# A batch's layer norm moved into the end of the scan stage, 64-row matmuls issued as halves, and one load delayed in the DMA queue

## The chip, the cores and the metric

One core of a Trainium2 chip runs the whole program. The metric is device time in microseconds (us), from start to end of one execution.

## What is computed

x has 4 batches of 64 channels and 32 x 32 positions (1024 tokens). Three parts follow one another, all in float32:

```python
# 1. two selective scans (forward, reversed), 128 inner channels, 16 states, for each of 4 batches
h = dA * h + (dt_t * x_t)[:, :, None] * B_t[:, None, :]   # over 1024 positions
y = jnp.einsum('bds,bs->bd', h, C_t)
y = _groupnorm_silu(y_f + y_b, gn_gamma, gn_beta) + x
# 2. causal attention over 1024 tokens, one head of 64
t = t + softmax(mask(q k^T / 8)) v,   q, k, v from layernorm(t)
# 3. spectral filter layer with hard expert choice (the first chosen expert adds up)
t = t + sum_k conv(layernorm(t), phi_k) (M_phi_plus_k, M_phi_minus_k) + 3 taps
```

## The kernel before, in words

The program has three blocks with a barrier between them; the order of work on each engine is written out by hand and tied by semaphores.

**Scan stage** (`mamba_stage`). A unit is one batch in one direction, so there are 8 units of 16 states. For a state the DMA queue (SP, `spread_b`, `spread_c`, line 388) copies a row of B and of C to all 128 partitions (`b_wide`, `c_wide`, 4 buffers each). VectorE (DVE) multiplies (`drive_step`, L1050; seven states of a unit get their drive from GpSimd or TensorE) and scans (`scan_step`, L1067). GpSimd (POOL) multiplies with C (`prod`, L479) and makes the shared drives (L467). TensorE (PE) sums the 16 products (`sum_states`, L591). ScalarE (ACT) makes exponentials. `store_sums` and `load_sums` (L140, L147) carry the group norm's sums through DRAM, in the same DMA queue. The last unit also holds batch 0's layer norm and its q, k and v. After its last state come `last_product` (L1094), `last_sum` (L597), `last_gate` (L1101), `last_out` (L606), and the copy `norm_take` (L778).

**Attention stage** (`attention_stage`). Four slots, one for each batch. A slot b attends batch b in 12 key blocks (`scores_t`, `exp`, `attend`), takes the row maxima of batch b+1 (`scores`, `reduce`, `maxima`), and normalizes and projects batch b+2 (`tokens`, `center_x`, `square`, `spread_x`, `rstd` on POOL, `norm_x`, `normed`, `queries`, `keys`; `values` in the slot after). Ahead of slot 0 stands a prologue: batch 0's maxima and batch 1's whole norm and q, k. In the prologue are also batch 3's group norm (`norm_squares` to `norm_silu`, with two table loads of ACT) and its residual on POOL (L1253). POOL meanwhile makes the expert matrices: `filter_rows`, `weigh_and_sum` (L1876, L1880), `even_matrices` (L1892), `odd_matrices`. Their weights come through the DMA queue behind `store_sums` and `load_sums`. The stage ends with a last norm chain of batch 3 (`rstd2(3)`, `norm_x2(3)`, `split_u(3)`, L1624) beside `taps_and_residual` (L1969) for batches 0 and 1.

**Filter stage** (`expert_stage`). For each of 2 pairs of batches, 16 filters: `convolve` (L2100) twice and `mix` (L1969) on PE, with ACT and DVE taking the results out. Pair 1's `taps_and_residual` stands between filters.

The projections of q and k contract 64 channels only: 64 rows of the array, outputs in two PSUM banks:

```python
for h in range(2):
    mm = nc.tensor.matmul(ps_p[:, h, :], w[:, :, :].rearrange("d j e -> d (j e)"),
                          halves(xn_t)[h], start=True, stop=True)
```

Of the kernel before, what the change touches and what calls it, by code (L numbers as in the profile page):

```python
# [22 lines left out]
ALU = mybir.AluOpType  # L23
# [3 lines left out]
B = 4  # L27
C = 64
# [23 lines left out]
ATTENTION_LOADS = 16 * (1 + 5)  # L52
# [6 lines left out]
BC_DEEP = 4  # L59
POOL_STATES = (2, 6, 9, 15)  # L60
# [19 lines left out]
def attention_tensors(nc, ctx):  # L80
# [11 lines left out]
    a.wq, a.wk = (sb(name, [C, 2, C]) for name in ("wq", "wk"))  # L92
    a.wv = sb("wv", [C, C])
# [7 lines left out]
    a.k_low = sb("k_low", [128, L], F32R)  # L101
    names = "zeros consts weights_in idents"
# [93 lines left out]
def mamba_stage(nc, ins, a, g, e, x1):  # L196
# [6 lines left out]
    with ExitStack() as ctx:  # L203
# [47 lines left out]
        xn_t = z_raw[0:C, :]  # L251
        cen, sq = (soft[:, j * H:(j + 1) * H].rearrange("p (i c) -> p i c", c=C) for j in range(2))
        xn = a.late[:, H:2 * H].rearrange("p (i c) -> p i c", c=C)
# [87 lines left out]
        with nc.Block() as block:  # L341

            @block.sync
            def _(sp):
# [23 lines left out]
                for w, name in ((a.wq, "Wq"), (a.wk, "Wk")):  # L368
                    for j in range(2):
                        sp.dma_start(w[:, j, :], ins[name]).then_inc(a.weights_in, 16)  # L370
                sp.dma_start(a.wv[:, :], ins["Wv"]).then_inc(a.weights_in, 16)
# [48 lines left out]
                spread_c(2 * B - 1, 1, N - 1)  # L420

            @block.gpsimd
            def _(pool):
# [31 lines left out]
                nc.gpsimd.tensor_tensor(e.sigma4[:, :], e.sigma[:, :], e.quarter[:, :], ALU.pow).then_inc(e.softmax_ready, 1)  # L455

# [12 lines left out]
                def batch(b, first=False, last=False):  # L469
                    for i in range(2):  # L470
                        u = 2 * b + i
                        for s in range(N):
# [20 lines left out]
                            if i == 1 and last and s == 4:  # L493
                                pool.wait_ge(ln_step, TOKEN_NORM)
                                nc.gpsimd.tensor_tensor(a.small[:, 2, :], a.small[:, 1, :], a.minus_half[:, :],
                                                        ALU.pow).then_inc(ln_rstd, 1)
# [7 lines left out]
                batch(B - 1, last=True)  # L504

            @block.tensor
            def _(pe):
# [160 lines left out]

                def tokens():
                    pe.wait_ge(g.squared_ready, B - 1)  # L670
                    scanned(2 * B - 1, LAST_SHARE[0])
                    for t in range(TILES):
                        delta, parity = divmod(t, 2)
                        mm = nc.tensor.transpose(ps_w[:, t * C:(t + 1) * C],
                                                 x1[:, SPAN * delta + parity:SPAN * (delta + 1):2], ident[0:C, 0:C])
                    mm.then_inc(tok_psum, 1)

                def normed():
# [3 lines left out]
                    for t in range(TILES):  # L682
                        mm = nc.tensor.transpose(ps_w[0:C, t * 128:(t + 1) * 128], xn[:, t, :], ident[:, :])
                    mm.then_inc(xnt_psum, 1)

                def queries_or_keys(w, done):
                    for h, out in enumerate(halves(ps_w)):
                        mm = nc.tensor.matmul(out, w[:, :, :].rearrange("d j e -> d (j e)"), xn_t[:, h * H:(h + 1) * H],
                                              start=True, stop=True)
                    mm.then_inc(done, 1)  # L690
# [26 lines left out]
                def values():  # L717
                    pe.wait_ge(k_ready, 1)
                    for t in range(TILES):
                        mm = nc.tensor.matmul(ps_w[:, t * C:(t + 1) * C], xn_t[:, t * 128:(t + 1) * 128], a.wv[:, :],  # L720
                                              start=True, stop=True)
                    mm.then_inc(v_psum, 1)
# [26 lines left out]
            def _(act):  # L749
# [109 lines left out]
                def square():  # L859
                    act.wait_ge(ln_step, 2)  # L860
                    nc.scalar.activation(sq, cen, ACT.Square).then_inc(ln_step, 1)

                def norm_x():
                    act.wait_ge(ln_rstd, 1)
                    for t in range(TILES):
                        part = nc.scalar.activation(xn[:, t, :], cen[:, t, :], ACT.Copy, scale=a.small[:, 2, t:t + 1])
                    part.then_inc(xn_ready, 1)

                def last_unit(u, i, s):
# [8 lines left out]
                    if s == 3:  # L878
                        square()
                        norm_silu(nc, act, g, B - 2)  # L880
                        nc.scalar.preload_act_table_set("natural_log_exp_and_others")
                    if s == 5:
                        norm_x()
                        scale_drive(u, LAST_TURNED[2], True)
                    if s == 6:
                        act.wait_ge(xnt_psum, 1)
                        nc.scalar.activation(xn_t, ps_w[0:C, :], ACT.Copy).then_inc(xnt_ready, 1)
# [15 lines left out]
                    if s == 15:  # L903
# [3 lines left out]
                        nc.scalar.activation(a.v_one[:, :, 0:C], ps_w[:, 0:H].rearrange("p (i c) -> p i c", i=TILES),  # L907
                                             ACT.Copy).then_inc(v_ready, 1)
# [102 lines left out]
                batch(B - 1, last=True)  # L1011
                norm_take(B - 1, ps_w)

            @block.vector
            def _(dve):
# [55 lines left out]
                def center_x():  # L1071

                    def chain(step, instruction):
                        instruction.then_inc(ln_step, 1)
                        dve.wait_ge(ln_step, step)

                    dve.wait_ge(tok_ready, 1)
                    chain(1, nc.vector.tensor_reduce(a.small[:, 0, :], a.tok, AX.X, ALU.add))
                    chain(2, nc.vector.scalar_tensor_tensor(out=cen, in0=a.small[:, 0, :].unsqueeze(2).to_broadcast([128, TILES, C]),
# [1208 lines left out]
```

## Time and profile before

| | us |
|---|---|
| median of 3 runs (912.4 to 916.39) | 915.15 |
| the profiled execution's own time | 911.7 |
| its span, first to last instruction | 909.9 |
| scan stage, about | 0 to 464 |
| attention stage, about | 464 to 612 |
| filter stage, about | 612 to 910 |

The rows of a timeline give the start in us, the length in us, the engine, the line, the operation with what it writes and reads, how often it stands there in a row, and in brackets the idle time before it and what ended that.

### The profile page before, as it was taken

To read this page: it belongs to the slowest core of one execution; us is meant where nothing else is said; L and a number is where in the kernel's file an instruction comes from. 1 tells how busy PE (TensorE), PEld (TensorE's weight loads), DVE (VectorE), ACT (ScalarE), POOL (GpSimd) and SP (SyncE) were. 2 spreads that over 40 slices of the span, in tenths; PEclk is the share of its full clock that TensorE was granted. 3 is DMA by queue.
4 is the path that set the end of the run, shared out by engine and by line. 5 is a ranking of instruction groups with operands and counts; after the bars stand their busy time and mean duration, and the time that the engine had idled before them with its cause. 6 is when DMAs were issued, how large, how long until landed. Compare 5 with 4: busy or idle time off the path is not lost. (4 is left out here: it accounts for less than half of the span.)

```text
span 909.9 us, 10954 instructions
## 1 busy us (share of the span) xinstructions
PE 823.3 (90%) x3238; PEld 505.1 (56%) x3238; DVE 677.8 (74%) x742; ACT 591.7 (65%) x941; POOL 536.5 (59%) x367
## 2 busy tenths in 40 slices
PE   5598899979999898977979999989999999999997
PEld 1243443434444343433435555558888888888886
DVE  2889999999989999998953664647666565565665
ACT  3887869788787979876626456556555554555554
POOL 4688989899998998887947952412121221212220
PEclk9699999999999999997987999999999999999999
DMA  6969897788959788694639300003334242243432
GB/s 150 342 225 320 276 303 267 310 294 301 308 200 387 262 299 316 251 331 165 232 44 158 104 1 1 1 1 93 124 107 139 92 139 94 93 139 96 135 107 78
DMA packets 72470, 165.67 MB, mean 182 GB/s; under 512 B 24194, under 2 KB 25236, under 8 KB 72420
## 3 DMA queue, kind: packets, MB, share of 16 engines
q1 hardware_dynamic: 72436, 165.27, 56.1%
q8 instruction: 15, 0.25, 0.1%
q14 instruction: 19, 0.16, 0.1%
HBM read 162.99 MB, written 2.26 MB: 182 GB/s over the span
## 5 line engine op out<-in xcount | busy, mean ns | idle before, releaser
L479 POOL TENSOR_TENSOR prod<-hidden,c_wide 128x1024 f32<-128x1024 f32 x127 | 298.1, 2361 | 43.3 <-DVE hidden L1067 35.8
L591 PE MATMUL ps_y<-prod,ident 128*128 128x512 f32 x508 | 239.6, 612 | 21.7 <-ACT ps_y L766 12.1
L1067 DVE TENSOR_TENSOR_SCAN hidden<-decay,ps_d 128x1024 f32<-128x1024 f32 x97 | 221.3, 2282 | 11.8 <-PE ps_d L582 3.3
L2100 PE MATMUL ps_conv<-hankel,u_high 128*128 128x512 f32 (+1 forms) x768 | 212.5, 358 | 0.1
L591 PEld LDWEIGHTS ps_y<-prod,ident 128*128 128x128 f32 x508 | 94.6, 194 | 141.3 <-issue 121.1
L2100 PEld LDWEIGHTS ps_conv<-hankel,u_high 128*128 128x128 f32 x768 | 138.5, 189 | 24.7 <-DVE u_t L1963 0.3
L2100 PE MATMUL ps_conv<-hankel,u_low 128*128 128x512 f32 (+1 forms) x384 | 137.2, 357 | 0.0
L1928 POOL CAST block_mix<-even 128x256 fp32r (+1 forms) x32 | 12.7, 397 | 204.9 <-PE sums L1969 204.9
L2217 DVE TENSOR_TENSOR stack<-ps_conv,stack 64x512 fp32r<-64x512 f32 x128 | 88.3, 690 | 60.2 <-ACT stack L2184 57.7
L2217 DVE TENSOR_TENSOR qk<-ps_conv,qk 64x512 fp32r<-64x512 f32 x128 | 88.2, 689 | 48.3 <-ACT qk L2184 45.7
L2184 ACT ACTIVATE stack<-ps_conv 64x512 fp32r<-64x512 f32 x128 | 76.0, 594 | 72.5 <-PE ps_conv L2100 70.6
L2184 ACT ACTIVATE qk<-ps_conv 64x512 fp32r<-64x512 f32 x128 | 76.0, 594 | 61.3 <-PE ps_conv L2100 59.3
L1050 DVE TENSOR_TENSOR ps_d<-ps_x,b_wide 128x1024 f32<-128x1024 f32 x73 | 89.9, 1232 | 7.5 <-DMA b_wide<-bc_rows 3.1
L467 POOL TENSOR_TENSOR drive<-dtx,b_wide 128x1024 f32<-128x1024 f32 x31 | 73.1, 2358 | 19.6 <-DMA b_wide<-bc_rows 19.5
L2100 PEld LDWEIGHTS ps_conv<-hankel,u_low 128*128 128x128 f32 x384 | 72.2, 188 | 12.7
L838 ACT ACTIVATE drive_t<-dtx_t,b_t 128x128 f32<-128x128 f32 x192 | 58.5, 387 | 2.1 <-PE ps_d L582 1.9
L1067 DVE TENSOR_TENSOR_SCAN hidden<-ps_w,drive 128x1024 f32<-128x1024 f32 x24 | 54.5, 2272 | 3.9 <-ACT ps_w L851 3.8
L845 ACT ACTIVATE decay<-dt_b,a_neg_b 128x1024 f32<-128x1024 f32 x49 | 53.8, 1138 | 3.3 <-DVE hidden L1067 3.0
L845 ACT ACTIVATE decay<-dt_f,a_neg_f 128x1024 f32<-128x1024 f32 x48 | 52.2, 1137 | 1.3 <-DVE dt_f L1027 0.9
L582 PE MATMUL ps_d<-ident,drive_t 128*128 128x128 f32 x192 | 28.2, 290 | 18.7 <-DVE hidden L1067 14.6
L1649 DVE TENSOR_REDUCE max_parts<-sums 128x1 f32<-128x512 f32 (+1 forms) x48 | 27.6, 598 | 22.7 <-PE sums L1325 13.5
L582 PEld LDWEIGHTS ps_d<-ident,drive_t 128*128 128x128 f32 x192 | 22.7, 147 | 35.5 <-DVE hidden L1067 17.6
(298 smaller groups left out, 1192.3 us busy)
## 6 DMA issues: line engine op xcount, KB each, us to landing
c_wide<-bc_rows SPq DMA_DIRECT2D x128, 512.0 KB, 4.7
b_wide<-bc_rows SPq DMA_DIRECT2D x104, 512.0 KB, 5.6
hankel<-filters SPq DMA_DIRECT2D x32, 1026.0 KB, 5.3
plus<-in_M_phi_plus SPq DMA_DIRECT2D x2, 1024.0 KB, 13.0
minus<-in_M_phi_minus SPq DMA_DIRECT2D x2, 1024.0 KB, 17.4
x_pair<-in_x SPq DMA_DIRECT2D x2, 768.0 KB, 9.2
bc_rows<-mixed_and_low SPq DMA_DIRECT2D x8, 128.0 KB, 4.0
out<-plus SPq DMA_DIRECT2D x8, 128.0 KB, 3.5
```

The source lines that it names most:

```text
L467: nc.gpsimd.tensor_tensor(drive[DRIVE_OF[s]][:, :], dtx[:, :], b_wide[slot][:, :], ALU.mult).then_inc(share_ready, 1)
L479: nc.gpsimd.tensor_tensor(prod[k % PAIR][:, :], hidden[k % DEEP][:, :], c_wide[s % BC_DEEP][:, :], ALU.mult).then_inc(prod_ready, 1)
L582: mm = nc.tensor.transpose(ps_d[:, t * 128:(t + 1) * 128], drive_t[:, t, :], ident[:, :])
L591: mm = nc.tensor.matmul(out, ident[:, :], halves(prod[k % PAIR])[h], start=False, stop=True, skip_group_check=True)
L838: part = nc.scalar.activation(drive_t[:, t, :], dtx_t[:, t, :], ACT.Copy, scale=b_t[:, t, s:s + 1])
L845: nc.scalar.activation(decay[decay_slot(s, last)][:, :], dt[i][:, :], ACT.Exp, scale=a_neg[i][:, s:s + 1]).then_inc(decay_ready, 1)
L1050: nc.vector.tensor_tensor(ps_d[:, :], ps_x[:, :], b_wide[slot][:, :], ALU.mult).then_inc(drive_ready, 1)
L1067: nc.vector.tensor_tensor_scan(hidden[k % DEEP][:, order], left[:, order], right[:, order], 0.0, ALU.mult, ALU.add).then_inc(hidden_ready, 1)
L1649: nc.vector.tensor_reduce(max_parts[:, i, at // H:at // H + 1], ps_s[c % 2][:, 0:n], AX.X, ALU.max, negate=True).then_inc(part_ready, 1)
L2100: mm = nc.tensor.matmul(out, pairs[q][wp][:, 2 * delta + source, :], rows, start=(delta == 0 and term == 0), stop=(delta == 2 * half + 1 a ...
L2184: nc.scalar.activation(stacks[slot][0:C, source, b, :, half * 2 * HEAD:(half + 1) * 2 * HEAD], ps_conv[source][lanes(b), half, :, :], ACT. ...
L2217: nc.vector.tensor_tensor(low, ps_conv[source][lanes(b), half, :, :], high.bitcast(F32), ALU.subtract).then_inc(conv_low, 1)
```

## The change

It has four parts.

1. Batch 1's layer norm leaves the attention prologue. PE turns its tokens into `ps_x` after the last drive has been read (`next_tokens`), DVE centers them behind `last_product` and spreads them ahead of `last_gate`, ACT squares, POOL takes the power as its last instruction in the stage, and DVE multiplies (`norm_next`) behind the gate. The attention stage starts with `normed(1)`. Its prologue is written anew: q, k and v of batch 1 and the first four key blocks of batch 0 stand between the score pieces. Batch 1's tokens are turned once more there, since the residual needs them in `tok`; batch 2's tokens come one key block later. Batch 3's SiLU with its table loads goes to block 6 of slot 0, its sums (`norm_squares`) behind `take_normed`, and POOL's list changes.
2. Row halves: the normed tokens lie as two halves of 512 on partitions 0 to 63 and 64 to 127 (`xn_t` 128 x 512), the weights are loaded twice, and the matmuls of the two halves alternate (`project_halves`, `value_halves`), in the attention stage in steps of 256 columns.
3. Column halves: in `taps_and_residual` the 16 residual matmuls write batch b to partitions 64 b to 64 b + 63, the two batches alternating.
4. `C_LATE = 2`: the queue issues the C row of state s - 2 behind the B row of state s, where it was that of s - 1.

```diff
-ATTENTION_LOADS = 16 * (1 + 5)
+ATTENTION_LOADS = 16 * (1 + 10)
+C_LATE = 2
...
+def project_halves(nc, banks, w, xn_t, step=SPAN):
+    for at in range(0, H, step):
+        for h in range(2):
+            rows = slice(h * C, (h + 1) * C)
+            mm = nc.tensor.matmul(banks[h][:, at:at + step], w[rows, :, :].rearrange("d j e -> d (j e)"),
+                                  xn_t[rows, at:at + step], start=True, stop=True)
+    return mm
+def value_halves(nc, banks, w, xn_t):
+    for t in range(TILES // 2):
+        for h in range(2):
+            rows = slice(h * C, (h + 1) * C)
+            mm = nc.tensor.matmul(banks[h][:, t * C:(t + 1) * C], xn_t[rows, t * 128:(t + 1) * 128], w[rows, :],
+                                  start=True, stop=True)
+    return mm
...
-                        if u or s:
-                            before, state = divmod(u * N + s - 1, N)
+                        if u * N + s >= C_LATE:
+                            before, state = divmod(u * N + s - C_LATE, N)
...
                     if k == 2 * N - 2:
+                        next_tokens()
                         last_out(0)
...
                 last_product()
+                center_next()
+                spread_x(1)
                 last_gate()
+                norm_next()
...
-                rstd(1)
                 filter_rows(nc, pool, e)
                 norm_rstd(nc, pool, g, a.minus_half, B - 1)
+                weigh_and_sum(nc, pool, e, 0, 3)
+                rstd(2)
+                weigh_and_sum(nc, pool, e, 3, EXPERTS + 2)
                 pool.wait_ge(g.act_ready, B)
                 nc.gpsimd.tensor_tensor(x1[:, (B - 1) * L:], g.mixed[:, :], x1[:, (B - 1) * L:], ALU.add).then_inc(g.x1_ready, 1)
-                weigh_and_sum(nc, pool, e, 0, EXPERTS + 2)
-                rstd(2)
                 weigh_and_sum(nc, pool, e, EXPERTS + 2, 2 * EXPERTS)
...
-                tokens(1)
+                normed(1)
                 scores(0, 0, 4)
                 maxima(0, 0, rows=0, back=0)
+                queries(1)
                 scores(0, 4, 6)
...
-                norm_squares(nc, act, g, B - 1, xn_t[:, :], g.mixed[:, :])
-                take_tokens(1)
-                square(1)
-                row(0, 0)
-                row(0, 1)
-                norm_x(1)
                 take_normed(1, 0)
                 take_normed(1, 1)
-                norm_silu(nc, act, g, B - 1)
-                nc.scalar.preload_act_table_set("natural_log_exp_and_others")
+                norm_squares(nc, act, g, B - 1, k_low[1][0:C, :], g.mixed[:, :])
+                row(0, 0)
+                take_q(1)
...
-    for b in range(2):
-        for a in range(2):
-            for delta in range(SPANS):
-                dst = (e.low[0:C, b, a, :], e.mid[0:C, b, a, :], e.tail[b][0:C, a, 0:HEAD],
-                       e.tail[b][0:C, a, HEAD:])[delta]
+    for a in range(2):
+        for delta in range(SPANS):
+            for b in range(2):
+                rows = lanes(b)
+                dst = (e.low[rows, b, a, :], e.mid[rows, b, a, :], e.tail[b][rows, a, 0:HEAD],
+                       e.tail[b][rows, a, HEAD:])[delta]
```

The first place is TensorE at the end of the scan stage, from the values of batch 0 on. Before:

```order
L720 MATMUL ps_w<-wv,z_raw 128x64 x8
L591 MATMUL ps_y<-prod,ident 128x512 x2
L606 MATMUL ps_w<-gated_f,packed_inner_f 64x512 x2
L591 MATMUL ps_y<-prod,ident 128x512 x2
L597 MATMUL ps_y<-prod,ident 128x512 x2
L606 MATMUL ps_w<-gated_b,packed_inner_b 64x512 x2
```

And now:

```order
L124 MATMUL ps_w<-wv,z_raw 128x64 x8
L619 MATMUL ps_y<-prod,ident 128x512 x2
L700 MATMUL ps_x<-ident,x 128x64 x8
L634 MATMUL ps_w<-gated_f,packed_inner_f 64x512 x2
L619 MATMUL ps_y<-prod,ident 128x512 x2
L625 MATMUL ps_y<-prod,ident 128x512 x2
L634 MATMUL ps_w<-gated_b,packed_inner_b 64x512 x2
```

One step of eight small matmuls (L700, batch 1's tokens) was put ahead of the first output product; nothing left the list.

The second place is POOL in the attention stage, from the filter rows to the end of the weighing (`small` is a norm's power, `gn` the group norm's, `x` the residual of batch 3). Before:

```order
L1234 TENSOR_TENSOR small<-small,minus_half 128x8
L1832 CAST even<-even 16x512
L169 TENSOR_TENSOR gn<-gn,minus_half 64x1
L1253 TENSOR_TENSOR x<-mixed_and_low,x 64x1024
L1876 TENSOR_TENSOR plus<-plus,w_sigma 128x1024 x2
...
L1880 TENSOR_TENSOR minus<-minus 128x1024
L1234 TENSOR_TENSOR small<-small,minus_half 128x8
...
L1892 TENSOR_TENSOR even<-plus,minus 128x1024 x4
L1238 TENSOR_TENSOR small<-small,minus_half 128x8
L1234 TENSOR_TENSOR small<-small,minus_half 128x8
```

And now:

```order
L191 TENSOR_TENSOR gn<-gn,minus_half 64x1
L1946 TENSOR_TENSOR plus<-plus,w_sigma 128x1024 x2
L1950 TENSOR_TENSOR plus<-plus 128x1024
L1946 TENSOR_TENSOR plus<-plus,w_sigma 128x1024
L1950 TENSOR_TENSOR plus<-plus 128x1024
L1289 TENSOR_TENSOR small<-small,minus_half 128x8
...
L1310 TENSOR_TENSOR x<-mixed_and_low,x 64x1024
...
L1962 TENSOR_TENSOR even<-plus,minus 128x1024 x4
L1293 TENSOR_TENSOR small<-small,minus_half 128x8
L1289 TENSOR_TENSOR small<-small,minus_half 128x8
```

The residual of batch 3 now stands inside the weighing instead of ahead of it, and batch 2's power stands after three of the eight matrices; the powers that batch 0's second norm and batch 3's norm need stand behind `even`, as they did.

The third place is the DMA queue at its start. Before:

```order
L371 DMA wv<-in_Wv 64x64
L376 DMA bc_rows<-mixed_and_low 32x1024
L388 DMA b_wide<-bc_rows 128x1024 x2
L388 DMA c_wide<-bc_rows 128x1024
L388 DMA b_wide<-bc_rows 128x1024
```

And now:

```order
L394 DMA wv<-in_Wv 64x64
L393 DMA wq<-in_Wq 64x64 x2
L393 DMA wk<-in_Wk 64x64 x2
L394 DMA wv<-in_Wv 64x64
L399 DMA bc_rows<-mixed_and_low 32x1024
L411 DMA b_wide<-bc_rows 128x1024 x3
L411 DMA c_wide<-bc_rows 128x1024 x2
```

Five loads of weights stand ahead of the first store of B and C rows, and each C row one B row later.

## Rows read from the trace of the kernel before

**Rows 1.** Chain that ended last: start, us, what.
```profile
616.53 7.28 PE ps_conv L2100 x36
...
762.24 6.49 PE sums L1969 x47
```

**Rows 2.** Windows, a stretch of the scan stage: busy us of each engine.
```profile
200.00:250.00 50.00, 47.78 (x138) 21.14 (x136) 48.63 (x28) 41.26 (x58) 48.13 (x22) 1.00 0.86 295
```

**Rows 3.** Timeline of PE, attention prologue and slot 0.
```profile
464.41 1.14 PE L1278 MATMUL sums<-ident,x 64*128 64x64 f32 x8 [1.61 <-PEq L341]
...
473.00 0.31 PE L1338 MATMUL ps_m<-ident_r,neg_max 128*66 128x128 f32 x2 [2.40 <-ACT qk L1511]
...
477.48 1.91 PE L1287 MATMUL sums<-ident,xn 128*64 128x128 f32 x8 [2.58 <-ACT xn L1470]
...
502.00 0.50 PE L1323 MATMUL sums<-block_mix 128*128 128x512 f32 x1
```

**Rows 4.** Windows, the prologue and slot 0's start: busy us of PE, granted clock, DMA.
```profile
464.00:500.00 36.00, 29.34 (x115) 0.76 1.12 125
```

**Rows 5.** Timeline of POOL, attention stage.
```profile
484.02 2.35 POOL L1253 TENSOR_TENSOR x<-mixed_and_low,x 64x1024 f32<-64x1024 f32 x1 [3.87 <-ACT mixed_and_low L189]
486.68 3.88 POOL L1876 TENSOR_TENSOR plus<-plus,w_sigma 128x1024 f32<-128x1024 f32 x2 [0.31 <-DMA plus<-in_M_phi_plus]
...
518.86 9.68 POOL L1892 TENSOR_TENSOR even<-plus,minus 128x1024 f32<-128x1024 f32 x4 [0.17 <-POOL minus L1880]
539.02 1.65 POOL L1238 TENSOR_TENSOR small<-small,minus_half 128x8 f32<-128x8 f32 x1 [10.49 <-DVE small L1620]
540.63 1.64 POOL L1234 TENSOR_TENSOR small<-small,minus_half 128x8 f32<-128x8 f32 x1
```

**Rows 6.** Timeline of DVE, end of the attention stage.
```profile
610.88 0.69 DVE L1624 TENSOR_TENSOR u_low<-u_all,u_high 128x512 fp32r<-128x512 f32 x1 [4.46 <-ACT u_high L1483]
```

**Rows 7.** Timeline of PE, end of the attention stage.
```profile
607.05 3.71 PE L1969 MATMUL sums<-ident,x 128*64 128x128 f32 x32
```

**Rows 8.** Timeline of PE, end of the scan stage.
```profile
451.48 2.00 PE L720 MATMUL ps_w<-wv,z_raw 64*128 64x64 f32 x16
453.41 1.98 PE L591 MATMUL ps_y<-prod,ident 128*128 128x512 f32 x4
455.32 1.93 PE L606 MATMUL ps_w<-gated_f,packed_inner_f 128*64 128x512 f32 x4
```

**Rows 9.** Timeline of DVE, the last gate of the scan stage.
```profile
460.13 1.48 DVE L1101 TENSOR_TENSOR gated_b<-ps_y,gate_b 128x512 f32<-128x512 f32 x2 [2.71 <-PE ps_y L597]
```

**Rows 10.** Timeline of ACT, attention stage.
```profile
464.24 1.06 ACT L133 ACTIVATE xn_t<-mixed_and_low 64x1024 f32<-64x1024 f32 x1 [0.29 <-PEq L341]
...
478.58 0.59 ACT L1489 ACTIVATE xn_t<-sums 64x512 f32<-64x512 f32 x1 [1.15 <-PE sums L1287]
...
542.80 2.02 ACT L1470 ACTIVATE xn<-cen,small 128x64 f32<-128x64 f32 x8
```

**Rows 11.** Timeline of PE, queries of batch 3.
```profile
549.83 1.98 PE L1293 MATMUL sums<-xn_t,wq 64*128 64x512 f32 x4 [0.61 <-ACT xn_t L1489]
```

**Rows 12.** Timeline of PE's weight loads, values of batch 1.
```profile
495.21 1.86 PEld L1308 LDWEIGHTS sums<-wv,xn_t 64*128 64x128 f32 x16 [0.38 <-issue]
```

**Rows 13.** Waits, scan stage from 40 to 450 us: total, times, longest.
```profile
DVE ps_d L1050 <- DMA b_wide<-bc_rows: 3.1, 3, 1.1
...
POOL prod L479 <- DVE hidden L1067: 34.5, 34, 4.3
```

**Rows 14.** Timeline of DVE, scan stage.
```profile
50.77 2.29 DVE L1067 TENSOR_TENSOR_SCAN hidden<-ps_w,drive 128x1024 f32<-128x1024 f32 x1 [3.31 <-ACT ps_w L851]
...
437.70 1.23 DVE L1050 TENSOR_TENSOR ps_d<-ps_x,b_wide 128x1024 f32<-128x1024 f32 x1
...
442.75 2.29 DVE L1067 TENSOR_TENSOR_SCAN hidden<-decay,ps_d 128x1024 f32<-128x1024 f32 x1
```

**Rows 15.** The spreads' line: issue to landing, all 232.
```profile
DMA to landing us min/median/max: 3.3/5.2/10.9
```

More of the change, by code:

```diff
@@ L419, in _ @@
                     unit(u, u % 2)
-                spread_c(2 * B - 1, 1, N - 1)
+                for state in range(N - C_LATE, N):
+                    spread_c(2 * B - 1, 1, state)
             @block.gpsimd
@@ L682, in normed @@
                     for t in range(TILES):
-                        mm = nc.tensor.transpose(ps_w[0:C, t * 128:(t + 1) * 128], xn[:, t, :], ident[:, :])
+                        mm = nc.tensor.transpose(ps_w[0:C, t * 128:(t + 1) * 128], xn[0][:, t, :], ident[:, :])
                     mm.then_inc(xnt_psum, 1)
                 def queries_or_keys(w, done):
[L687 to L690, printed above, removed]
+                    project_halves(nc, halves(ps_w), w, xn_t, step=H).then_inc(done, 1)
                 def queries():
@@ L718, in values @@
                     pe.wait_ge(k_ready, 1)
[L719 to L722, printed above, removed]
+                    value_halves(nc, halves(ps_w), a.wv, xn_t).then_inc(v_psum, 1)
                 first_attention = {3: tokens, 7: normed, 10: queries, 11: queries_rest, 12: keys, 13: keys_rest, 15: values}
@@ L886, in last_unit @@
                         act.wait_ge(xnt_psum, 1)
-                        nc.scalar.activation(xn_t, ps_w[0:C, :], ACT.Copy).then_inc(xnt_ready, 1)
+                        for h, part in enumerate(halves(ps_w)):
+                            taken = nc.scalar.activation(xn_t[h * C:(h + 1) * C, :], part[0:C, :], ACT.Copy)
+                        taken.then_inc(xnt_ready, 1)
                         shared_decay_of(u, i, LAST_SHARE[2], xnt_ready, 1, True)
@@ L1291, in project @@
                 def project(w, done):
-                    for h in range(2):
-                        mm = nc.tensor.matmul(ps_p[:, h, :], w[:, :, :].rearrange("d j e -> d (j e)"),
-                                              halves(xn_t)[h], start=True, stop=True)
-                    mm.then_inc(done, 1)
+                    project_halves(nc, [ps_p[:, h, :] for h in range(2)], w, xn_t).then_inc(done, 1)
                 def queries(b):
@@ L1306, in values @@
                     pe.wait_ge(k_ready, b)
-                    for i in range(TILES):
-                        mm = nc.tensor.matmul(ps_p[:, 0, i * C:(i + 1) * C], xn_t[:, i * 128:(i + 1) * 128], a.wv[:, :],
-                                              start=True, stop=True)
-                    mm.then_inc(v_psum, 1)
+                    value_halves(nc, [ps_p[:, h, :] for h in range(2)], a.wv, xn_t).then_inc(v_psum, 1)
                 def scores(b, lo, hi):
@@ L1433, in _ @@
                 scores(0, 6, 8)
-                normed(1)
+                keys(1)
+                scores_t(0, 0)
+                scores_t(0, 1)
                 scores(0, 8, 10)
                 maxima(0, 2, rows=2, back=0)
+                values(1)
+                attend(0, 0)
+                scores_t(0, 2)
                 scores(0, 10, 12)
-                queries(1)
-                scores_t(0, 0)
-                scores_t(0, 1)
-                keys(1)
+                attend(0, 1)
+                scores_t(0, 3)
                 maxima(0, 3, rows=3, back=0)
-                for b in range(B):
+                attend(0, 2)
+                tokens(1)
+                scores_t(0, 4)
+                attend(0, 3)
+                scores_t(0, 5)
+                slot(0, begun=4)
+                for b in range(1, B):
                     slot(b)
@@ L1691, in slot @@
                         output(b - 1, 3)
[L1692 removed]
+                    if ahead and b:
                         take_values(b + 1)
```

177 lines of the change are left out of this document (108 added, 69 removed).

## The prediction

> **What bounds the kernel now.** I read the chain that ended last first: from 616.53 on it is PE alone, some 7 us of `convolve` and then `mix`, in turn [rows 1], to the end of the span of 909.9. Whatever PE no longer does there comes off the time one for one. Then the windows of the scan stage: in 50 us DVE is busy 48.6 and POOL 48.1 [rows 2], so DVE sets the pace and POOL is close behind. In the attention stage the reader should look for PE's idle time: it waits 2.40 and 2.58 us for ACT, which waits for batch 1's norm, and the row of slot 0 that I compare by, the third score piece of batch 1, starts at 502.00 [rows 3]; over 36 us PE is busy 29.3 and its granted clock is 0.76 on average, that is, half of the time at the lower of its levels of 1.2 and 2.4 GHz [rows 4]. POOL looks free there, since it waits 10.49 us at 539.02, but its list is in order and begins only when the first expert matrices land, at 486.68 [rows 5]. The stage ends with DVE at 611.57 [rows 6], 0.8 us after PE at 610.76 [rows 7].
>
> **The tail of the scan stage: +0.6 us.** PE has no gap from the values of batch 0 to the last output product [rows 8]. Eight small matmuls are put in. They cost 1.14 us in the same form in [rows 3]; starts follow one another some 0.07 closer, so 1.07. The values ahead of them (2.00, [rows 8]) get 0 to 1.0 shorter by the row halves; I take 0.5. That makes +0.6, bounds +0.1 and +1.1. DVE's part (two operations behind `last_product`, a square on ACT, two more ahead of the gate) is some 3 us of work in the gap of 2.71 us before the gate [rows 9], so it may add 0.3. POOL's power (1.65, [rows 5]) and `norm_next` lie beside the last product and `norm_take`.
>
> **The prologue of the attention stage: what PE could win.** At least the two waits, 5.0 us [rows 3]. At most 36.0 - 29.3 x about 0.77 = 13.4 us, which is the whole stretch without a wait at full clock [rows 4]. Laid out by hand with the rows' durations (first four pieces as before to 469.2; queries to 470.7; keys from 473.7, when ACT and DVE have taken q; values from 477.7; then only PE work), the fourth key block ends at about 486.0. Slot 0 gives some back: batch 2's tokens come a block later, DVE centers them ahead of its first reductions, and the third score piece starts at about 492 in place of 502.00: 10 us. Batch 3's SiLU with its two table loads (about 3.8 us on ACT) moves to block 6, where ACT is two blocks ahead; I cost it at nothing, and 3.8 is the price if that cover is gone. q, k and v of batch 2 add some 2 us by the halves, and batch 2's power, now behind three matrices on POOL, takes about 1 back. So PE would arrive at batch 3's norm some 11 us early.
>
> **What POOL allows: -6.6 us.** Batch 3's norm needs POOL's power behind `even`. POOL was idle there 10.49 us and now is not. First, `norm_squares` stands behind PE's eight transposes (464.41 to 465.5) and the copy of their second half (0.59), so it starts at 466.2 and not at 464.24 [rows 3, 10]: the store of the sums, and every load of expert weights behind it in the DMA queue, is 2.0 us late, and so is 486.68. Second, batch 3's residual (2.35) stood ahead of the landing, where it cost nothing, and now stands behind it [rows 5]. `even` ended at 528.54 and now ends at 528.54 + 2.0 + 2.35 = 532.9. Two powers follow, 1.61 and 1.64, to 536.2. `norm_x` of batch 3 started at 542.80 [rows 10] and starts at 536.2: -6.6, whatever PE won. ACT, and PE behind it at `normed`, wait for POOL there, a wait of about 4 us in place of the ones removed. The bounds are 5.0 (if PE wins only its two waits) and 11 (if POOL isn't late at all).
>
> **Row halves behind that point: -2.1 us.** Batch 3's q and k are 1.98 each, its v 2.00 [rows 11, 8]; nothing in the trace runs two matmuls on different rows of the array, so the bounds are 0 and half of each. q and k now are 8 matmuls of 256 columns each with a weight load; 16 such loads took 1.86, so 8 take 0.93 [rows 12], which fits beside halved matmul time (0.99). I take 0.8 off each. Values are 16 loads in 1.86 us, so the loads set their 2.00; if these don't overlap, nothing is won: I take 0.5. Together 2.1, bounds 0 and 3.0. Only batch 3's count, since those of batches 1 and 2 are absorbed in POOL's lateness. The Trainium skill (TensorEngine Tiling, Tiling Modes) says that different tiles can load weights and multiply in parallel, which would give the upper bound, 3.0, and that changing the tiling mode drains TensorE, which speaks against small groups between full-size ones; no row here shows either.
>
> **Column halves: -1.5 us.** 32 matmuls take 3.71 us [rows 7]; 0 to 1.85 off. I take 1.5, since at 0.116 us apiece other fixed costs will show. For pair 0 it buys nothing: the stage ends with DVE's norm chain, 0.8 us after PE [rows 6, 7]. For pair 1 it lies in the filter stage's chain (within the 6.49, [rows 1]) and counts whole. If PE's longer idle time, now some 2.5 us, drops its clock for the first `convolve`, that costs up to 1.7; I leave it out of the sum.
>
> **C one state later, and five more loads: 0.** All that DVE ever waits for B rows is 3.1 us, three times right behind the group norm's store and load, which stay where they are [rows 13]. So at most -3.1, and I take 0. The price is a C row's lead. Behind B rows whose buffer is freed by the drive three states back, C of a state is now issued when the drive ends at 438.93 and its product can start when the scan ends at 445.04: 6.1 us [rows 14], against a landing of 5.2 at the median and 10.9 at most [rows 15]. POOL may come some us late once in a unit, and it has 34.5 us of waits for DVE over 8 units, 4.3 each [rows 13]. The five loads stand ahead of the first store; a microsecond there is covered by DVE's 3.31 us wait for ACT at 50.77 [rows 14].
>
> **Sum.** +0.6 - 6.6 - 2.1 - 1.5 + 0 = -9.6. The profiled execution took 911.7 and would take 902.1; that run was 3.4 under the median of 915.15, so I forecast 915.15 - 9.6 = 905.5.
>
> **Rivals.** (1) The halves don't overlap: PE does the same work in order. For it speaks that no row shows overlap. The tail then costs 1.1: +1.1 - 6.6 = -5.5, 909.6. Chance 0.15. (2) POOL isn't the bound: its chain is earlier than I think, or PE wins more of its lead back later. Then the 11 count: about -14, 901. Against it speaks that POOL's list is fixed and dense [rows 5]. Chance 0.12. (3) The late C rows turn the scan stage slower. In each unit a landing near the 10.9 of [rows 15] makes POOL 4.8 late against 4.3 of slack, 0.5 each, 4 in all: -5.6. From 11.6 us of landing in every unit on (10.9 + 0.7, then 1.2 each and 9.6 in all) the gain is gone, and at 13.5 it is 3.1 a unit, 25 us of delay, and the kernel is 15 slower. For it: POOL is busy 96% in [rows 2]. Against: the median landing is inside the lead. Chance 0.12, about a third of it past the sign: 930. (4) SiLU and its table loads in slot 0 stop PE for their 3.8. They end before POOL's bound, so nothing changes; only together with rival 2 they count.
>
> The forecast itself has 0.61. A measurement of this kernel tells about 0.5%, 4.6 us, from no change. Faster by more than that (under 910.6): the forecast, rival 2, most of rival 1, and the mild half of rival 3, less what run-to-run spread takes: 0.82. Within 0.5%: 0.13. Slower: 0.05. The range of 8 in 10 goes from rival 2's 901 to just past rival 1's 909.6: 900.5 to 911.
>
> **What would show it.** In the profile after: eight matmuls into `ps_x` ahead of the output product and the attention stage starting about 0.6 later; no wait of PE for ACT's `xn` in the prologue; the third score piece of batch 1 near 492.5; the first `plus` operation of POOL near 489; ACT's `norm_x` of batch 3 waiting for POOL and starting near 536.5 to 537; q and k near 1.2 us and not 1.98; the 32 residual matmuls near 2.2 and not 3.71; the filter stage's stretches of `convolve` unchanged at about 7. Wrong it would be if DVE shows new waits for POOL products in the scan stage, if the halves' rows keep their length, or if `norm_x` of batch 3 does not wait for POOL.

## The result, and the profile after

The changed kernel takes 908.45 us (median of 6 runs, 907.12 to 909.92), the kernel before on the same chip 915.37 (6 runs, 912.4 to 917.22). The ratio is 0.9926, with a 95% interval from 0.9905 to 0.9947: 6.9 us faster, where 9.6 were forecast. Between the two profiled executions (911.7 and 907.5) the difference is 4.2, and the readings below are made against that.

Timeline of PE in the changed kernel, from the end of the scan stage to the start of the filter stage:

```profile
452.79 1.11 PE L124 MATMUL ps_w<-wv,z_raw 64*128 64x64 f32 x16
...
455.74 1.17 PE L700 MATMUL ps_x<-ident,x 64*128 64x64 f32 x8
...
465.94 1.03 PE L1343 MATMUL sums<-ident,xn 128*64 128x128 f32 x8 [1.61 <-PEq L363]
...
491.43 0.50 PE L1373 MATMUL sums<-block_mix 128*128 128x512 f32 x1 [1.92 <-DVE max_parts L1720]
...
506.34 1.91 PE L1343 MATMUL sums<-ident,xn 128*64 128x128 f32 x8 [4.59 <-ACT xn L1530]
...
527.93 1.04 PE L1420 MATMUL ps_o<-probs,v_one 128*65 128x512 f32 x2 [1.51 <-ACT o_t L1584]
...
536.92 0.31 PE L1430 MATMUL ps_m<-ident,o_t 65*128 65x65 f32 x2 [2.23 <-DVE x L1750]
...
543.78 1.06 PE L1343 MATMUL sums<-ident,xn 128*64 128x128 f32 x8 [0.29 <-ACT xn L1530]
...
548.87 1.13 PE L114 MATMUL sums<-xn_t,wq 64*128 64x256 f32 x8 [0.73 <-ACT xn_t L1548]
...
552.39 1.13 PE L114 MATMUL sums<-xn_t,wk 64*128 64x256 f32 x8
...
558.38 1.11 PE L124 MATMUL sums<-wv,xn_t 64*128 64x64 f32 x16
...
603.32 1.97 PE L2039 MATMUL sums<-ident,x 128*64 128x128 f32 x32
608.53 1.73 PE L2019 MATMUL ps_conv<-ident,u_all 128*128 128x128 f32 x8 [3.24 <-PEq L1277]
```

The attention stage starts at 465.94, 1.5 later than before. The two waits of the old prologue are gone, and the third score piece starts at 491.43 where it was 502.00 [rows 3]: PE has won more than 10 us. Part of that is the clock: over 464 to 500 PE is busy 31.19 us at a granted clock of 0.95, where it was 29.34 at 0.76 [rows 4]:

```profile
464.00:500.00 36.00, 31.19 (x166) 19.59 (x166) 20.57 (x58) 19.84 (x31) 18.24 (x15) 0.95 0.97 109
```

Then three new waits stand out: 4.59 for batch 2's `xn`, 1.51 for ACT's `o_t` and 2.23 for DVE's `x`. Behind the last one the granted clock is 0.75 on average over the 6.9 us to batch 3's norm, where it was 1.00 in the kernel before, and PE takes 6.86 us for the stretch (536.92 to 543.78) that took 5.26 before (539.61 to 544.87). At batch 3's norm (543.78, before 544.87) only 1.1 of the 10 is left. q, k and v of batch 3 and the residual are short now: 1.13, 1.13, 1.11 and 1.97, for 1.98, 1.98, 2.00 and 3.71 [rows 7, 8, 11].

The chain that ended last shows pair 1's taps and residual, 4.75 for 6.49 [rows 1]. Its first `convolve` holds 54 matmuls, where the chain before had only 36 of them, so the two lengths can't be compared; the first `mix` can. It starts 13.0 behind the stage's start (621.55 - 608.53), where it was 11.75 (623.65 - 611.90):

```profile
610.26 11.46 PE ps_conv L2171 x54
...
760.14 4.75 PE sums L2039 x47
```

POOL in the attention stage, to be laid beside [rows 5]:

```profile
491.76 3.88 POOL L1946 TENSOR_TENSOR plus<-plus,w_sigma 128x1024 f32<-128x1024 f32 x2 [7.73 <-DMA plus<-in_M_phi_plus]
...
502.58 1.66 POOL L1289 TENSOR_TENSOR small<-small,minus_half 128x8 f32<-128x8 f32 x1
...
523.73 2.36 POOL L1950 TENSOR_TENSOR minus<-minus 128x1024 f32<-128x1024 f32 x1
526.26 9.90 POOL L1962 TENSOR_TENSOR even<-plus,minus 128x1024 f32<-128x1024 f32 x4 [0.17 <-POOL minus L1950]
536.33 1.65 POOL L1293 TENSOR_TENSOR small<-small,minus_half 128x8 f32<-128x8 f32 x1 [0.17 <-DVE small L1690]
537.95 1.64 POOL L1289 TENSOR_TENSOR small<-small,minus_half 128x8 f32<-128x8 f32 x1
```

The expert weights landed 5.1 later than before. Batch 2's power stands behind three matrices, so it started at 502.58, while DVE's part of that norm had been done at 493.81; that is PE's wait of 4.59. POOL then works with hardly a gap from 491.76 to 539.59. What DVE does beside it:

```profile
493.64 0.17 DVE L1672 TENSOR_SCALAR small<-small 128x8 f32<-128x8 f32 x1
...
523.50 0.67 DVE L1682 TENSOR_REDUCE small<-x 128x8 f32<-128x512 f32 x1
524.21 2.43 DVE L1683 SCALAR_TENSOR_TENSOR cen<-small,x 128x512 f32<-128x512 f32 x1
...
529.56 0.69 DVE L1665 SCALAR_TENSOR_TENSOR cen<-small,sums 128x512 f32<-128x512 f32 x1
...
531.34 0.33 DVE L1739 TENSOR_SCALAR neg_max<-max_parts,neg_max 128x1 fp32r<-128x1 f32 x2
...
532.98 0.79 DVE L1672 TENSOR_SCALAR small<-small 128x8 f32<-128x8 f32 x1
533.68 0.67 DVE L1688 TENSOR_REDUCE small<-u_all 128x8 f32<-128x512 f32 x1
534.39 1.80 DVE L1690 TENSOR_SCALAR small<-small 128x8 f32<-128x8 f32 x1
```

In the kernel before, the same four operations of slot 1 were:

```profile
530.88 0.69 DVE L1613 SCALAR_TENSOR_TENSOR cen<-small,x 128x512 f32<-128x512 f32 x1
...
537.91 0.17 DVE L1602 TENSOR_SCALAR small<-small 128x8 f32<-128x8 f32 x1
537.99 0.68 DVE L1618 TENSOR_REDUCE small<-u_all 128x8 f32<-128x512 f32 x1
538.71 0.17 DVE L1620 TENSOR_SCALAR small<-small 128x8 f32<-128x8 f32 x1
```

What counts here is their length, not a wait ahead of them. The same `TENSOR_SCALAR` takes 0.17, 0.79 and 1.80. Each long one ends just behind the end of an operation of POOL: 526.64 behind 526.09; 533.77 and 536.19 behind the ends of the third and the fourth operation of `even` (four operations of some 2.47 each from 526.26, so 533.7 and 536.16). The reductions between them keep their 0.67, and the same `SCALAR_TENSOR_TENSOR` keeps its 0.69 when its second operand lies in PSUM (529.56). The two `TENSOR_SCALAR` on a single element per partition also keep their length (0.33 for both, at 531.34), though they run beside `even` too. In the kernel before, DVE did these steps between 530.88 and 538.88, while POOL sat in its idle 10.49 us [rows 5]. The three stretches add 1.74, 0.62 and 1.63: 4.0 us on DVE's path. PE feels the first through ACT, which takes `o_t` behind DVE's centered tokens (the wait of 1.51), and the other two in the wait of 2.23 for `x`, which stands behind them.

The Trainium skill (SBUF — State Buffer, Who interferes with whom) says that DVE and GpSimd share one port pair, and that whichever issues first keeps it for the whole instruction. A DVE operation with two inputs in SBUF contends for it with a GpSimd instruction that reads SBUF. `tensor_scalar` can contend too, when its operands let it enter a fast two-port mode, and a reduction never does on this chip. The rows above agree with it; whether a given `TENSOR_SCALAR` was in such a mode, no row shows. Such a hold isn't new: in the kernel before, batch 2's `TENSOR_SCALAR` took 1.60 at 504.21 and ended 0.03 behind an operation of POOL, but POOL came to that norm's power only at 508.31.

ACT's norm of batch 3:

```profile
541.31 0.37 ACT L1572 ACTIVATE qk<-ps_m 2x256 fp32r<-2x256 f32 x1 [5.92 <-PE ps_m L1388]
541.71 2.02 ACT L1530 ACTIVATE xn<-cen,small 128x64 f32<-128x64 f32 x8
```

It starts at 541.71 (before 542.80), and it does not wait for POOL, whose power was ready at 539.59; ACT had been waiting for PE until 541.31.

### The profile page after: what moved, and what is told of

It is laid out like the page before. It is cut to its first block and busy times, and to the rows that moved or that the text cites. A ratio compares the mean times of both kernels' runs of the same rounds, so it can differ in the third digit from the quotient of the medians.

```text
span 905.7 us, 11019 instructions
## 1 busy us (share of the span) xinstructions
PE 809.3 (89%) x3270; PEld 499.5 (55%) x3270; DVE 680.9 (75%) x743; ACT 590.1 (65%) x935; POOL 536.5 (59%) x367
```

## Experiments

All are compared with the kernel before by the ratio of the medians. "Changed" is the kernel of the result above, 0.9926 [0.9905, 0.9947].

**1. POOL's powers ahead of `even`.**

```diff
-                even_matrices(nc, pool, e)
                 rstd2(0)
                 rstd(3)
+                even_matrices(nc, pool, e)
```

> Against the changed kernel (908.45 median, profile 907.5) one thing differs: POOL's two powers of slot 1 (batch 0's second norm, batch 3's norm) stand ahead of the four even matrices and not behind them; POOL does the same work. Theory A (POOL's running instruction holds up DVE): in the changed kernel two of DVE's small operations took 0.79 and 1.80 us where 0.17 is usual, and each ended where one of POOL's even operations ended (533.68 and 536.16). With POOL waiting for DVE instead, both are 0.17 again, PE's wait of 2.23 for DVE's x and the stretch at half clock behind it go, and norm_x of batch 3 starts near 538.5 and not at 541.71: 2.5 to 3.5 us faster, about 905.5 median. Theory B (my prediction's: only the time of POOL's power counts): the power was ready at 539.59 and ACT took it up 2.1 later, so an earlier power buys nothing: 0, DVE's rows keep their length. Theory C (PE's low clock is the cause of the late arrival): DVE's rows are short again but norm_x stays within 1 us of 541.7.

Measured: 904.48, ratio 0.9884 [0.9865, 0.9902], 4.0 faster than the changed kernel. DVE and POOL in slot 1:

```profile
525.05 2.41 DVE L1683 SCALAR_TENSOR_TENSOR cen<-small,x 128x512 f32<-128x512 f32 x1
...
534.05 0.17 DVE L1672 TENSOR_SCALAR small<-small 128x8 f32<-128x8 f32 x1
...
534.85 0.17 DVE L1690 TENSOR_SCALAR small<-small 128x8 f32<-128x8 f32 x1
```

```profile
535.16 1.65 POOL L1293 TENSOR_TENSOR small<-small,minus_half 128x8 f32<-128x8 f32 x1 [8.25 <-DVE small L1690]
```

The two operations that lay beside `even` are 0.17 again, the third, which still lies beside the weighing, keeps its 2.41, and `norm_x` of batch 3 starts at 538.95. The work of POOL is the same, only its place differs. Theory A holds; B and C fall. PE's rows bear out the size: from its wait for `o_t` to batch 3's norm PE takes 12.27 (528.75 to 541.02), where it took 15.85 (527.93 to 543.78). The wait of 2.23 is gone, and the last stretch takes 5.27 at a granted clock of 1.00, where it took 6.86 at 0.75. The first hold is still there, and so is PE's wait for `o_t` (1.49). The rows of batch 2 show how much of this is timing: its `TENSOR_SCALAR` took 0.17 in the changed kernel, where it fell on the seam between two operations of POOL, and 1.84 here, with the same neighbours.

**2. Plus matrices ahead of the sums in the DMA queue.**

```diff
+                load_expert_part(sp, ins, e, 0)
                 store_sums(sp, g, B - 1)
                 load_sums(sp, g, B - 1)
-                load_expert_weights(sp, ins, e)
+                load_expert_part(sp, ins, e, 1)
+                store_filters(sp, e)
```

Part 0 is the filter rows' input and the plus matrices, part 1 the minus matrices and the taps.

> Against the changed kernel: the loads of phi and of the plus matrices are issued ahead of the store and load of batch 3's group norm sums and no longer behind them, so they leave at about 466 in place of 473.1. Theory: POOL's first plus operation starts near 484 in place of 491.76, batch 2's power (behind three matrices) is ready as soon as DVE is (near 495.5 in place of 504.2), so PE's wait of 4.59 for batch 2's xn goes. Even then runs from about 518 to 528 and meets fewer of DVE's small operations of slot 1 near 530. Expected 3 to 6 us faster, near 904. Rival: the sums' load now lands behind the plus matrices, batch 3's group norm becomes late by several us, and DVE, which stands in order behind it, takes the gain back: 0 or slower.

Measured: 901.37, ratio 0.9841 [0.9822, 0.9861], 7.1 faster than the changed kernel, more than expected. POOL starts `plus` at 488.23 and not at 484. It doesn't wait for the matrices there; its list has the group norm's power ahead of them, and the sums now land later (POOL waits 9.79 there). Even so batch 2's power comes 3.6 earlier (499.03), and `normed(2)` starts at 503.85 with a wait of 0.30 where it was 4.59. The rival's delay of the group norm was there (DVE waits 2.33 for it) but stopped nothing of PE's. DVE's holds beside `even` are still there (0.90 and 1.80). And here the prediction's wait appears: ACT's `norm_x` of batch 3 is released by POOL's power, if after only 0.27 us:

```profile
536.27 2.02 ACT L1532 ACTIVATE xn<-cen,small 128x64 f32<-128x64 f32 x8 [0.27 <-POOL small L1291]
```

This profile also shows the hold the other way round. DVE's operation with two inputs in SBUF started first and kept its 0.69, and POOL's took 2.84 instead of some 2.36:

```profile
520.12 0.69 DVE L1685 SCALAR_TENSOR_TENSOR cen<-small,x 128x512 f32<-128x512 f32 x1
```

```profile
520.22 2.84 POOL L1957 TENSOR_TENSOR minus<-minus 128x1024 f32<-128x1024 f32 x1
```

**3. Both.**

> Both edits, powers ahead of even and plus loads ahead of the sums. If POOL's lateness (4.59 at batch 2's norm) and POOL's hold on DVE (about 3.9 in slot 1) are two separate losses, this is the fastest of the three: 5 to 8 us under the changed kernel, 901 to 903. If one hides the other, it is no faster than the better of the two alone.

Measured: 896.3 (5 runs, 895.44 to 897.14), ratio 0.9792 [0.9773, 0.9811]: 12.2 faster than the changed kernel, beyond what I expected and about the sum of the two (4.0 and 7.1). The first hold is nearly gone too (1.03 for 2.43), and with it PE's wait for `o_t`. Windows of the attention stage, busy us of PE, PEld, DVE, ACT and POOL, then the granted clock, the DMA share and GB/s, first of the changed kernel and then of this one:

```profile
500.00:545.00 45.00, 34.50 (x173) 21.13 (x171) 24.52 (x55) 20.52 (x46) 43.64 (x22) 0.92 0.32 68
```

```profile
500.00:545.00 45.00, 41.18 (x222) 24.69 (x222) 27.16 (x65) 30.50 (x68) 38.84 (x19) 1.00 0.20 54
```

```profile
532.95 1.06 PE L1345 MATMUL sums<-ident,xn 128*64 128x128 f32 x8 [0.30 <-ACT xn L1532]
```

PE's idle time in these 45 us falls from 10.5 to 3.8, and PE is at batch 3's norm at 532.95, 11.9 ahead of the kernel before. The prediction had PE arrive "some 11 us early" if POOL allowed it.

**4. The same two edits on the kernel before.**

> The kernel before with the two edits that helped the changed one (POOL's powers ahead of even, plus loads ahead of batch 3's sums). Theory A: in the kernel before POOL was no bound (it waited 10.49 for DVE) and held no small operation of DVE long, so the edits win nothing there: within 1 us of before; the bound is one that the change made. Theory B: they are gains by themselves, 5 to 10 us.

Measured: 920.8, ratio 1.0078 [1.0053, 1.0102], 7 us slower. Neither theory of this experiment had this. The kernel before has DVE's `norm_stats` of batch 3 ahead of its last reductions, in order:

```profile
486.66 0.18 DVE L161 TENSOR_REDUCE gn<-gn_group 64x2 f32<-64x32 f32 x1 [10.66 <-DMA gn_group<-gn_rows]
```

```profile
487.97 0.80 PE L1325 MATMUL sums<-qk 128*128 128x512 f32 x1 [6.03 <-DVE max_parts L1651]
```

DVE waits 10.66 for the late sums, and PE 6.03 for the reductions behind them. In the changed kernel these steps stand behind the reductions, which is why the late landing costs nothing in experiment 2. So the two edits together are no gain by themselves. That they remove a bound which the change had made fits this, but the powers' new place was not tried alone on the kernel before, and its `TENSOR_SCALAR` of 1.60 (above) shows that POOL did hold DVE once there, against what was expected.

**5. The halves one after the other.**

```diff
-    for at in range(0, H, step):
-        for h in range(2):
+    for h in range(2):
+        for at in range(0, H, step):
```

The values' loop is turned in the same way.

> The changed kernel, but the matmuls of the two row halves no longer alternate: all of the first 64 rows, then all of the other 64, in q, k and v; same count, same columns. Theory A (two matmuls run at once when they stand next to one another on different rows): q and k go back from 1.13 to about 1.98 and values from 1.11 to about 2.0. Batch 3's three come whole: about 2.4 us slower than the changed kernel (near 910.9). Theory B (256 columns instead of 512, or the halves' layout, make them short): they stay near 1.1 and the time stays.

Measured: 908.37, ratio 0.9892 [0.9864, 0.992], not to be told from the changed kernel. Batch 3's q and v:

```profile
549.65 1.14 PE L114 MATMUL sums<-xn_t,wq 64*128 64x256 f32 x8 [0.75 <-ACT xn_t L1548]
...
559.20 1.60 PE L124 MATMUL sums<-wv,xn_t 64*128 64x64 f32 x16
```

Values went half way back, q not at all. That left open whether q's gain is overlap.

**6. 256 columns on one row group**, in the kernel before (one execution, 912.48):

> The kernel before with q's and k's matmuls of batches 1 to 3 in steps of 256 columns, all on the same 64 rows. Theory A (the halves' 1.13 comes from two row groups that run at once, even where their four and four matmuls follow one another): q and k stay at 1.98 here. Theory B (the smaller step makes them short): they take about 1.14 here.

```profile
550.59 1.99 PE L1294 MATMUL sums<-xn_t,wq 64*128 64x256 f32 x8 [0.62 <-ACT xn_t L1490]
```

The same eight matmuls on one row group take 1.99. So the second row group makes the gain, not the smaller step, and alternating isn't needed for it where a run on one group is four matmuls long.

**7. Pair 0's residual in turn.**

```diff
-    for a in range(2):
-        for delta in range(SPANS):
-            for b in range(2):
+    order = [(a, delta, b) for a in range(2) for delta in range(SPANS) for b in range(2)] if q else \
+        [(a, delta, b) for b in range(2) for a in range(2) for delta in range(SPANS)]
+    for a, delta, b in order:
```

> The changed kernel, but pair 0's 32 residual matmuls, the last of PE in the attention stage, do not alternate between the column halves (pair 1's still do). Expected: 3.71 in place of 1.97, PE ends 1.7 later, at about 607.0, still ahead of DVE's end of 608.20, so the filter stage starts at the same 608.5. Theory A: PE's idle time before it, 3.24 in the changed kernel, is what drops its clock for the first eight transposes and the first convolve (1.73 and the steps behind it, 1.3 us longer than before); with 1.5 of idle time the clock stays and this kernel is about 1.3 faster than the changed one. Theory B: that low clock was a chance of the one profile (other variants had 1.06 with an idle time of 2.9): no difference.

Measured: 904.83, ratio 0.9861 [0.9833, 0.9889], 3.6 faster than the changed kernel.

```profile
602.49 3.33 PE L2039 MATMUL sums<-ident,x 128*64 128x128 f32 x32
607.35 1.06 PE L2019 MATMUL ps_conv<-ident,u_all 128*128 128x128 f32 x8 [1.53 <-PEq L1277]
...
619.11 2.01 PE L2039 MATMUL sums<-qk,block_mix 128*128 128x256 f32 x10
```

The first mix starts 11.76 behind the stage's start, against 13.0 in the changed kernel (621.55 - 608.53), where the granted clock is 0.55 over the first 2.5 us. The longer residual costs nothing, as the stage waits for DVE. In this profile 1.25 of the 2.4 us between the spans (903.3 and 905.7) come from there; 1.1 come from the scan stage, whose code is the same. The rest of the 3.6 is not explained by any row.

**8. Both edits of experiment 3 and this one.**

> Powers ahead of even, plus loads ahead of the sums, C two states late, and pair 0's residual matmuls not alternating (896.3 median without the last). Theory A: PE's idle time of 2.88 ahead of the filter stage is what costs the first convolve 1.25 (first mix 13.0 behind the stage's start, against 11.75 where the idle time was 1.14, 1.53 and 1.83); with the residual 1.4 longer and hidden, this kernel is 1.2 faster: 895. Theory B: the 1.25 is chance: same time.

Measured: 896.53, ratio 0.9808 [0.9785, 0.9831]: the same as experiment 3 within the intervals. The profile has the filter stage 1.2 shorter (894.9 - 598.93 = 295.97 against 894.7 - 597.57 = 297.13), while its scan stage ended 1.7 later. Over all thirteen profiles, PE's idle time ahead of the filter stage was 1.14 or 1.15 (four times), 1.53 (twice) and 1.83, with the first mix 11.75 or 11.76 behind the stage's start; where it was 2.88 to 3.24, the mix came after 13.0 in five cases and after 11.75 in one. So the mechanism is shown in the profile, not at every execution; the medians don't tell 1.2 us.

**9. The queue's order alone**, on the kernel before (`C` rows two states late):

> The kernel before with the queue's order alone changed: each C row is issued two states late in place of one. In the profiles so far the steps of DVE behind the group norm's load (state 11 of units 2, 4 and 6) take 4.62, 4.45 and 4.74 with C one state late and 3.66 each with two: 2.8 in all. But the changed kernel gives 1.0 to 2.3 us each back in steps of units 3, 5 and 7, where DVE waits for ACT, ACT for PE, and PE's sums took 3.75 in place of 1.95 (half clock, behind an idle time of 3.86 in place of 3.64). Theory A: those stretches come with the queue's order (the timing inside a unit moves, and PE's idle time with it); then this kernel's last scan starts near 455.1 as in the changed kernel and the time is that of before or 1 slower. Theory B: they come with something else of the change, or are chance; then the last scan starts near 451.0 and the kernel is 2.8 us faster than before.

Measured: 913.23, ratio 0.9963 [0.9942, 0.9985]: 3.4 faster, interval 1.4 to 5.3. DVE's waits for `b_wide` are gone. But the profile shows no gain: the last scan starts at 452.94, 0.9 earlier than before, yet the first scan had started 1.35 earlier (26.32 for 27.67), so the stretch between them is 426.62 for 426.14, and the profiled executions take 911.6 and 911.7. Neither theory is borne out as a whole. The medians' 3.4 stands, but where it comes from is not shown.

**10. C one state late again**, in the changed kernel:

> Against the changed kernel: the C row is again one state late in the queue (C_LATE = 1). The changed kernel's last product of DVE ended its scans 1.3 us later than before (457.44 against 456.13), with 5.0 us more of DVE's waits for ACT and 3.1 less for B rows. Theory A: the queue's order is the cause of the 1.3; then this kernel's last product starts near 456.1, DVE waits 3.1 for b_wide again, and it is about 1.3 faster than the changed one. Theory B: the five further weight loads or chance alignment make the 1.3; then it stays at 457.4 or later, and the wait for b_wide comes on top: 0 to 3 us slower than the changed kernel.

Measured: 908.61, ratio 0.9923 [0.9903, 0.9944]. The waits of DVE for B rows are back:

```profile
DVE ps_d L1086 <- DMA b_wide<-bc_rows: 3.2, 3, 1.2
```

The last scan starts 3.5 later than in the changed kernel, yet the medians are equal.

**11. C one state late in the kernel of experiment 3.**

> The fastest kernel so far (powers ahead of even, plus loads ahead of the sums; 896.3 median) with C one state late again. Theory A: two states late is worth the 2.8 us of the three steps: this one is 2 to 3 slower, near 899. Theory B: what it wins there it gives back in PE's low clock and the waits for ACT behind it: same time within 1.

Measured: 898.17, ratio 0.9805 [0.9776, 0.9834], 1.9 slower than experiment 3, and within the intervals the same.

Why the scan stage is so uneven is seen in PE's rows, first of the changed kernel and then of experiment 7, whose scan code is the same:

```profile
197.60 3.75 PE L619 MATMUL ps_y<-prod,ident 128*128 128x512 f32 x4 [3.86 <-ACT ps_y L797]
```

```profile
198.12 1.96 PE L619 MATMUL ps_y<-prod,ident 128*128 128x512 f32 x4 [3.92 <-ACT ps_y L797]
```

Behind almost the same idle time the same sums run once at a granted clock of 0.50 and once at 1.00. ACT waits for the projection behind them, DVE for ACT, and the steps of DVE from 204.17 to 210.86 take 6.69, where they take 4.39 (204.69 to 209.08) in experiment 7: 2.3 lost. From the first scan to the last, seven profiles with the changed kernel's scan code and two-state order range from 426.67 to 429.64 us. The kernel before has 426.14, and experiments 4 and 6, which run the very same scan stage, 428.35 and 428.04.

## Why the prediction came out as it did

**Direction and range held**; the sum did not: of its three gains two were right and the largest was mostly missing. In the profiles the filter stage starts 3.4 earlier, its first `mix` comes 1.3 later behind that, and pair 1 wins 1.7: with 0.4 at the program's end that is the 4.2. That the median came out 6.9 faster, well inside the range, is partly luck, as the profiled pair shows less and a scan stage with the same code varies by 3 us.

- **Tail, +0.6:** PE's rows bear it out on the low side. Values are 1.11 for 2.00, tokens 1.17, the gate has no new wait; from the last scan to the stage's start the tail grew by 0.2 (465.94 - 455.12 = 10.82, before 464.41 - 453.81 = 10.60).
- **"What PE could win":** right. Third score piece forecast near 492, found at 491.43; no wait for `xn` in the prologue. SiLU and its table loads in slot 0 stopped nothing, as rival 4 had it.
- **"What POOL allows: -6.6 us":** this step failed. The gain there was 1.1 from `norm_x` to `norm_x`, or 2.6 counted from the stage's start. Of the 5.5 between the forecast 536.2 and the 541.71 found, 3.4 is POOL's own lateness (its power was ready at 539.59) and the other 2.1 is PE's. The right engine was named, but only one of its ways to cost time was priced. First, the plus matrices landed 5.1 late, not 2.0: 1.5 from the later stage start, 2.0 from `norm_squares`, and most of the rest between issue and landing (17.3 for 16.0). Second, batch 2's power behind three matrices was priced at "about 1 back" and cost 4.6, because the landing was late; experiment 2 took it away. Third, POOL's busy stretch moved over DVE's norm chain and held three operations, 4.0 us; the prediction had no term for that, and experiment 1 took 2.25 of it away. Fourth, PE's clock fell behind the new waits (1.6 us behind the one of 2.23), which had no term either. In the end ACT did not wait for POOL at batch 3's norm at all, which the prediction had named as a sign that it was wrong.
- **Rival 2 (POOL isn't the bound, near 901):** it did not happen, but experiment 3 shows its size: without most of POOL's hold and lateness the kernel takes 896.3.
- **Row halves, -2.1:** the mechanism was right, the term slightly small. q, k and v of batch 3 fell by 0.85, 0.85 and 0.89, 2.6 in all. PE's lead over the kernel before grows from 1.1 at `normed(3)` to 3.5 at the score block behind the values (559.42 for 562.93). Rival 1 is out. The Trainium skill's rule on parallel tiles (TensorEngine Tiling (Array Packing), Tiling Modes) says that tiles can load weights and multiply in parallel, and this is borne out (16 values with 16 loads take 1.11 for 2.00); of its warning on a drain at a change of mode no row shows a cost: the next full-size matmul starts at 549.93, inside q's last one.
- **Column halves, -1.5:** 1.74 for pair 1 (6.49 to 4.75). For pair 0 "nothing" was right, and the low clock that was left out of the sum came: up to the first `mix` it cost 1.3.
- **C late, 0:** by itself it is 3.4 faster by the medians (interval 1.4 to 5.3), which the bound of -3.1 allows to that accuracy, but the profile of experiment 9 doesn't show the gain. In the changed kernel no difference could be measured. Rival 3, late C rows that slow the stage, did not show: POOL waits 5.6 for `c_wide` in all (3.4 before), and of POOL's products DVE waits for 0.4.
- **The rest is unevenness.** The changed kernel's last scan started 1.3 later in its profile. Since the same scan code ends anywhere within 3 us, I do not put that down to the change. It may also be why the profiles differ by 4.2 and the medians by 6.9.

## What to carry to other kernels

When work is moved forward in time, lay the other engines' busy stretches beside the new place and ask what each small operation now runs next to: a list of large GpSimd operations can hold a DVE operation with two inputs in SBUF, and even a `TENSOR_SCALAR` of 128x8, to the end of the one that runs. Put GpSimd's bulk work behind the small result that others wait for, and in the DMA queue put the loads of the longest list first; but check which in-order engine stands waiting for the load that became late (experiment 4 lost 7 us so). And judge edits worth a few us by the stage's own rows, since a stage nobody touched moved by 3 us.

## What the runs showed of the hardware

- Halves of the array, 64 rows or 64 columns each, overlap even when their matmuls don't alternate. Residual, values and q take 3.71, 2.00 and 1.98 on one group, and 3.33, 1.60 and 1.14 when one half follows the other. At 0.116, 0.125 and 0.248 us apiece that is some 3.3, 3.2 and 3.4 operations run beside the other half's in each case: an overlap of a few operations at the seam, counted in operations and not in time. This reading rests on these three rows.
- Whichever of DVE and GpSimd started first kept its length, and the other was held: 2.43, 0.79 and 1.80 for 0.69, 0.17 and 0.17 on DVE, and 2.84 for 2.36 on GpSimd (experiment 2).
- Two runs of the same code can differ in TensorE's granted clock behind the same idle time (0.50 and 1.00 behind 3.86 and 3.92), and where other engines wait for what comes next that costs 2.3 us.
